# Turning the next batch's mask half a tile apart, splitting the pairs' weights on GpSimd, and signalling the rows to gather first, in a routed expert kernel

## Chip, cores and metric

The kernel runs on one core of one Trainium2 chip. The metric is device time in microseconds (us) of the whole program; the lower the better.

## What is computed

For each of 4 batches the reference builds a 1024 x 1024 matrix `adj = side * cond * softmax(x) / 32`, puts minus infinity on its diagonal, and makes a 0/1 mask of the 10240 largest entries. The mask is the input of a mixture-of-experts layer, whose output is added to `x`:

```python
out = jnp.zeros((g, n * n), dtype=adj.dtype).at[rows, idx].set(1.0)     # the mask
...
scores = jax.nn.softmax(jnp.einsum('bsh,he->bse', x, G), axis=-1)       # x is the mask here
value, indices = jax.lax.top_k(scores, TOPK)                            # TOPK = 2 of E = 8
w = jnp.einsum('bsk,bske->bse', value, onehot)
gate = jax.nn.silu(jnp.einsum('bsh,efh->bsef', x, gate_w))
up = jnp.einsum('bsh,efh->bsef', x, up_w)
out = jnp.einsum('bsef,bse,ehf->bsh', gate * up, w, down_w)
lr = jnp.einsum('bsh,erh->bser', x, lora_A)
out = out + LORA_SCALE * jnp.einsum('bser,bse,ehr->bsh', lr, w, lora_B)
```

## The kernel before

The four batches run one after the other. The 2048 pairs (token, chosen expert) of a batch are sorted by expert into T = 23 tiles of 128 slots. A tile i goes through these steps:

- GpSimd (POOL) gathers its 128 mask rows from `mask_rows` in memory to `xg` (`gather`, L509, three buffers).
- TensorE (PE) turns them (`turn_x`, L663), ScalarE (ACT) copies the turned rows to `xt` (`store_xt`, L835).
- PE does the first layer (`first_layer`, L676, 16 matmuls), ACT the silu (L840), VectorE (DVE) the gating (`gate`, L1336 to L1344), PE turns that (`turn_g`, L687), DVE copies it (`store_gt`, L1352).
- PE does the second layer (`second_layer`, L699 to L702, 8 matmuls of 512 columns in two halves), ACT copies each half to `y` (`store_y`, L848, two buffers of y, each free again when its put has landed), and POOL scatters y to `put_rows` (`put_out`, L517).

PE's order is written out by hand. In its step i stand the first layer of tile i, the turn of x of tile i + 2, the turn of g of tile i - 1 and the second layer of tile i - 2; between these are spots 0 to 3, at which tables put work for batch n + 1. ACT and DVE have spots too. Each engine works strictly down its own list, so a wait at a spot holds all that is behind it.

In the spots of batch n the mask of batch n + 1 is made, ending with `check_mask` on DVE at (18, 2), which signals `mask_ready`. SyncE (SP) then loads x for a later batch (8 loads of 512 KB to `v`) and stores the mask (2 MB, L386). From tile 19 on, the mask is turned and scored, piece c of 8 at a time: PE turns it to one PSUM bank (`turn_mask`, L625), ACT copies that to `mt` (`store_mt`, L828, two buffers), PE multiplies by the router's weights (`score`, L632). The turn of piece c + 1 waits for the copy of piece c, since there is one bank. The score of piece 7 stands behind the last tile's step and signals `scores_ready`. DVE meanwhile takes row maxima of x of batch n + 2 (L931, table MAX_AT), each of which waits for its load.

`route(n + 1)` is then one long row of small DVE instructions, with a drain between any two that depend: `choose` (L1217, waits for `scores_ready` and for the mask's store, because it writes over the mask), `weigh` (the pairs' two weights, split into three fp16 parts each), `place_pairs` (each pair's tile and slot within it), `fill_table` (L1303, 1840 values for each partition), then 16 matmuls on PE (L652), and `take_slots` (the rows to gather and to put, and the scales, of all 23 tiles), which ends in the signal `routed`. POOL issues the first gather of the next batch only behind `routed`. The first batch's route runs once before the loop.

Behind the put of the last tile, SP loads the finished rows in pieces (L362, L364); POOL sums them (L526, L529) between the tiles of the next batch.

## Time and profile before

| what | us |
|---|---|
| median of 3 runs (lowest, highest) | 834.33 (832.57, 835.94) |
| profiled execution, its own time | 836.23 |
| its span in the trace | 834.5 |
| PE busy, DVE busy, ACT busy, POOL busy | 529.9, 519.5, 455.4, 388.8 |

The span is what the instructions of the profiled execution cover; 1.7 us of its time lie around it. No engine is busy for more than two thirds of the span, so the time is in waits, and the chain of work that ended last has to be read by stages. The TensorE clock that was granted was 0.838 of full speed on the mean.

### The profile page before, as it was taken

How to read it: one execution, taken by the hardware profiler on the slowest of the kernel's cores; microseconds unless marked ns; L12 is line 12 of the kernel's file. 1: busy time of each engine (PE TensorE's matmuls, PEld its weight loads, DVE VectorE, ACT ScalarE, POOL GpSimd, SP SyncE). 2: the span in 40 equal slices, each digit the busy share in tenths (PEclk: the TensorE clock that was granted, in tenths of full speed). 3: DMA queues.
4: the chain of work that ended last, by engine and by line, in shares of the span. 5: the costliest groups of instructions: out<-in, count | busy, mean ns of one | idle time of the engine just before them, and what ended most of it. 6: DMA issues, size and time to landing. Idle time of an engine off the chain costs nothing.

```text
span 834.5 us, 14610 instructions
## 1 busy us (share of the span) xinstructions
PE 529.9 (63%) x4178; PEld 358.9 (43%) x4178; DVE 519.5 (62%) x1242; ACT 455.4 (55%) x655; POOL 388.8 (47%) x337
## 2 busy tenths in 40 slices
PE   0211376289888754787887726987788368798810
PEld 0200365156555533454555414654455146465500
DVE  5768799576778465865885676757861623233335
ACT  6686387658744564485444553874445345355510
POOL 7123200234473114487786124877871157767510
PEclk9755599589999995898899967999999869899965
DMA  9980340114232904478377734685678247767569
GB/s 315 358 234 0 115 189 26 45 55 158 88 127 86 356 28 129 147 252 288 107 263 240 319 104 148 215 287 174 212 247 334 77 131 252 268 212 264 203 234 380
DMA packets 80443, 159.93 MB, mean 192 GB/s; under 512 B 22889, under 2 KB 32105, under 8 KB 79856
## 3 DMA queue, kind: packets, MB, share of 16 engines
q1 hardware_dynamic: 59760, 108.60, 37.8%
q0 software_dynamic: 20608, 50.37, 17.3%
q8 instruction: 43, 0.70, 0.4%
q14 instruction: 32, 0.26, 0.1%
HBM read 107.53 MB, written 73.40 MB: 217 GB/s over the span
## 4 chain that ended last, share of the span: by engine, by line
DMA 19%; PE 18%; DVE 17%; issue 15%; POOL 14%; ACT 8%; DVEq 4%; SPq 3%; POOLq 1%; ACTq 0%
DMA out_dram<-piece 7%; DMA piece<-put_rows 6%; PE pa L676 5%; ACT mask L791 3%; DMA xg<-mask_rows,where 3%; POOL piece L526 3%; POOL piece L529 3%; DVE mask L1060 3%; DVE w L1166 2%; PE pb L663 2%; POOL xg L509 2%; ACT t_row L828 2%; DMA w<-put_rows 2%; PE pd L625 2%; POOL put_rows L517 2%
## 5 line engine op out<-in xcount | busy, mean ns | idle before, releaser
L676 PE MATMUL pa<-w,xt 128*128 x1472 | 203.2, 294 | 1.1 <-issue 0.9
L848 ACT ACTIVATE y<-pc,where 128x512 f32<-128x512 f32 x184 | 125.3, 687 | 104.8 <-PE pc L702 97.4
L676 PEld LDWEIGHTS pa<-w,xt 128*128 128x128 f16 x1472 | 150.7, 103 | 62.1 <-issue 14.7
L517 POOL DMA_INDIRECT put_rows<-y,where x92 | 92.5, 1005 | 151.9 <-ACT y L848 133.3
L1336 DVE SCALAR_TENSOR_TENSOR g_full<-pa,where,s_act 128x144 f32<-128x144 f32 x92 | 33.5, 365 | 197.0 <-ACT s_act L840 196.9
L509 POOL DMA_INDIRECT xg<-mask_rows,where x92 | 97.4, 1058 | 122.8 <-DVEq L1328 92.9
L835 ACT ACTIVATE xt<-pb 128x1024 f16<-128x1024 f16 x92 | 94.3, 1025 | 101.7 <-PE pb L663 98.7
L663 PE MATMUL pb<-ident,xg 128*128 128x128 f16 x736 | 61.4, 231 | 68.5 <-DMA xg<-mask_rows,where 46.2
L663 PEld LDWEIGHTS pb<-ident,xg 128*128 128x128 f16 x736 | 48.7, 104 | 80.1 <-DMA xg<-mask_rows,where 53.5
L840 ACT ACTIVATE s_act<-pa,small 128x128 f32<-128x128 f32 x92 | 33.8, 368 | 86.8 <-PE pa L676 86.8
L702 PE MATMUL pc<-lb,gt 128*128 x184 | 77.4, 420 | 0.0
L701 PE MATMUL pc<-wd,gt 128*128 x184 | 77.3, 420 | 0.0
L700 PE MATMUL pc<-wd,gt 128*128 x184 | 77.2, 420 | 0.0
L699 PE MATMUL pc<-wd,gt 128*128 x184 | 76.9, 418 | 0.2 <-issue 0.2
L526 POOL TENSOR_TENSOR piece<-piece 128x512 f32<-128x512 f32 x48 | 60.9, 1269 | 30.1 <-DMA piece<-put_rows 29.6
L791 ACT ACTIVATE mask<-v,small 128x1280 f16<-128x1280 f32 x48 | 65.1, 1356 | 7.0 <-POOL v L465 3.8
L529 POOL TENSOR_TENSOR piece<-piece 128x512 f32<-128x512 f32 x48 | 62.8, 1308 | 3.8
L931 DVE TENSOR_REDUCE small<-v 128x1 f32<-128x1024 f32 x32 | 38.4, 1213 | 16.0 <-DMA v<-in_x_dram 15.7
L1344 DVE TENSOR_TENSOR g_parts<-g_full,g_parts 128x144 f16<-128x144 f32 x92 | 43.4, 472 | 6.8
L1004 DVE TENSOR_SCALAR_CACHE_REDUCE mask<-v,small 128x1024 f16<-128x1024 f32 x36 | 45.0, 1274 | 2.8 <-POOL v L465 2.1
L1352 DVE COPY gt<-pb 128x384 f16<-128x384 f16 x92 | 32.3, 351 | 22.6 <-PE pb L687 20.9
L951 DVE SCALAR_TENSOR_TENSOR v<-v,small,t_row 128x1024 f32<-128x1024 f32 x32 | 45.4, 1457 | 0.7
(208 smaller groups left out, 880.0 us busy)
## 6 DMA issues: line engine op xcount, KB each, us to landing
piece<-put_rows SPq DMA_DIRECT2D x96, 256.0 KB
v<-in_x_dram SPq DMA_DIRECT2D x40, 512.0 KB, 9.1
piece<-in_x_dram SPq DMA_DIRECT2D x48, 256.0 KB
out_dram<-piece SPq DMA_DIRECT2D x48, 256.0 KB, 3.8
mask_rows<-mask SPq DMA_DIRECT2D x4, 2048.0 KB, 16.6
w<-put_rows SPq DMA_DIRECT2D x16, 512.0 KB, 10.2
w<-in_L_ffn_gate_w_dram SPq DMA_DIRECT2D x8, 512.0 KB, 10.2
w<-in_L_ffn_up_w_dram SPq DMA_DIRECT2D x8, 512.0 KB, 8.3
```

The source lines that it names most:

```text
L509: pool.indirect_dma_start(out=xg[:, g % NX, :], out_offset=None, in_=mask_rows[n % 2], in_offset=bass.IndirectOffsetOnAxis(ap=mask_row[n][ ...
L517: pool.indirect_dma_start(out=put_rows[n % 2], out_offset=bass.IndirectOffsetOnAxis(ap=put_row[n][:, i:i + 1], axis=0), in_=y[:, g % NY, : ...
L526: nc.gpsimd.tensor_tensor(piece[:, at, 0, :], piece[:, at, 0, :], piece[:, at, 1, :], ALU.add).then_inc(half_summed, 1)
L529: nc.gpsimd.tensor_tensor(piece[:, at, 0, :], piece[:, at, 0, :], piece[:, at, 2, :], ALU.add).then_inc(summed_piece, 1)
L663: last = pe.transpose(xt_ps[:, t, :], xg[:, g % NX, t * P:(t + 1) * P], ident[:, :])
L676: last = pe.matmul(l1[g % 2], xt[:, g % 2, t, :], w1[:, bass.ds(e, 1), t, k, :].rearrange("p o n -> p (o n)"), start=(t == 0 and k == 0), ...
L700: pe.matmul(pc[:, half, :], high, own(wd[:, bass.ds(e, 1), 1, cols]), start=False, stop=False)
L701: pe.matmul(pc[:, half, :], low, own(wd[:, bass.ds(e, 1), 0, cols]), start=False, stop=False)
L702: pe.matmul(pc[:, half, :], lora, own(lb[:, bass.ds(e, 1), cols]), start=False, stop=True).then_inc(y_done, 1)
L791: nc.scalar.activation(mask[:, cols], v_flat[:, cols], ACT.Sign, bias=t_at[k - 1], scale=-1.0, accum_out=act_cnt[:, p:p + 1]).then_inc(act ...
L835: nc.scalar.activation(xt[:, g % 2, :, :], xt_ps, ACT.Copy).then_inc(xt_ready, 1)
L848: nc.scalar.activation(y[:, g % NY, half * HALF:(half + 1) * HALF], pc[:, half, :], ACT.Copy, scale=y_scale[n][:, i:i + 1]).then_inc(y_rea ...
```

## The change

Four edits are made.

1. The turns of the next batch's mask begin at (18, 3), behind the second layer of tile 16, and go on half a tile apart; ACT gets a spot ahead of its copy of x, where the copy of the turned mask now stands in every other case. The counts on ACT keep their places (their spots are numbered one higher).
2. `weigh` computes the two weights of a token and signals; the split into three parts (3 casts, 2 subtractions) is made on POOL (`cut_weights`), between the puts of the last two tiles. `fill_table` waits for it. What doesn't depend on the probabilities is moved ahead of the wait for them.
3. `place_pairs` finds tiles from the bits of a slot number that is biased by 2^23, in place of scaling and rounding.
4. `take_slots` computes the rows to gather first and signals `rows_ready`; the scales come behind, and `routed` after them. POOL's first three gathers wait for `rows_ready` alone.

```diff
-    TURN_AT = {(19, 0): 0, (19, 2): 1, (20, 0): 2, (20, 2): 3, (21, 0): 4, (21, 2): 5, (22, 0): 6, (22, 2): 7}
-    STORE_MT_AT = dict(TURN_AT)
+    TURN_AT = {(18, 3): 0, (19, 0): 1, (19, 3): 2, (20, 0): 3, (20, 3): 4, (21, 0): 5, (21, 3): 6, (22, 0): 7}
+    STORE_MT_AT = {(18, 3): 0, (19, 0): 1, (19, 3): 2, (20, 0): 3, (20, 3): 4, (21, 0): 5, (21, 3): 6, (22, 0): 7}
...
+            def cut_weights(n):
+                at = WEIGH_STEPS * n
+                pair = w_pair.rearrange("p (c r) -> p c r", c=C)
+                pool.wait_ge(weights_ready, n + 1)
+                for k in range(PARTS):
+                    if k > 0:
+                        pool.wait_ge(weighed, at + 2 * k)
+                    nc.gpsimd.tensor_copy(vals[:, :, :, 1 + k], pair).then_inc(weighed, 1)
+                    if k < PARTS - 1:
+                        pool.wait_ge(weighed, at + 1 + 2 * k)
+                        nc.gpsimd.tensor_tensor(pair, pair, vals[:, :, :, 1 + k],
+                                                ALU.subtract).then_inc(weighed, 1)
+            cut_weights(0)
             for n in range(B):
-                pool.wait_ge(routed, n + 1)
+                pool.wait_ge(rows_ready, n + 1)
                 pool.wait_ge(mask_stored, 16 * (n + 1))
                 for i in range(NX):
                     gather(n, i)
+                pool.wait_ge(routed, n + 1)
...
-                for i in range(T - 3, T):
-                    put_out(n, i)
+                put_out(n, T - 3)
+                put_out(n, T - 2)
+                if n + 1 < B:
+                    cut_weights(n + 1)
+                put_out(n, T - 1)
...
                     silu(n, i)
+                    between(i, 0)
                     if i + 2 < T:
                         store_xt(n, i + 2)
-                    between(i, 0)
+                    between(i, 1)
...
             def weigh(n):
                 V.tensor_scalar(power, row_count, 1.0, None, ALU.max)
+                for r in range(ROLES):
+                    V.tensor_scalar(vals[:, :, r, 0], token_1, float(r * S), None, ALU.add)
                 dve.drain()
...
                 V.tensor_scalar(power, power, 2.0, None, ALU.mult)
+                dve.drain()
+                V.reciprocal(unpower, power)
                 dve.wait_ge(probs_ready, n + 1)
...
                 V.reciprocal(z_sum, z_sum)
-                dve.drain()
-                V.scalar_tensor_tensor(z_sum, z_sum, LIFT, power, ALU.mult, ALU.mult)
+                V.tensor_copy(vals[:, :, :, 4], unpower.unsqueeze(2).to_broadcast([P, C, ROLES]))
                 dve.drain()
                 pair = w_pair.rearrange("p (c r) -> p c r", c=C)
-                V.tensor_copy(pair[:, :, 0], z_sum)
-                V.tensor_tensor(pair[:, :, 1], z_sum, w_second, ALU.mult)
-                V.reciprocal(power, power)
-                dve.drain()
-                for k in range(PARTS):
-                    V.tensor_copy(vals[:, :, :, 1 + k], pair)
-                    if k < PARTS - 1:
-                        dve.drain()
-                        V.tensor_tensor(pair, pair, vals[:, :, :, 1 + k], ALU.subtract)
-                        dve.drain()
-                for r in range(ROLES):
-                    V.tensor_scalar(vals[:, :, r, 0], token_1, float(r * S), None, ALU.add)
-                V.tensor_copy(vals[:, :, :, 4], power.unsqueeze(2).to_broadcast([P, C, ROLES]))
+                V.scalar_tensor_tensor(pair[:, :, 0], z_sum, LIFT, power, ALU.mult, ALU.mult)
+                dve.drain()
+                V.tensor_tensor(pair[:, :, 1], pair[:, :, 0], w_second, ALU.mult).then_inc(weights_ready, 1)
...
-                V.tensor_scalar(n_tiles, ranks[:, C, :], 1.0 / P, (P - 1) / (2.0 * P), ALU.mult, ALU.add)
-                dve.drain()
-                V.tensor_scalar(n_tiles, n_tiles, TO_WHOLE, None, ALU.add)
-                dve.drain()
-                V.tensor_scalar(n_tiles, n_tiles, -TO_WHOLE, None, ALU.add)
+                V.tensor_scalar(n_slots, ranks[:, C, :], P - 1.0 + WHOLE, None, ALU.add)
+                dve.drain()
+                V.tensor_scalar(bits(n_slots), bits(n_slots), -P, None, ALU.bitwise_and)
...
-                V.tensor_scalar(slot_tile, slot, 1.0 / P, -(P - 1) / (2.0 * P), ALU.mult, ALU.add)
-                dve.drain()
-                V.tensor_scalar(slot_tile, slot_tile, TO_WHOLE, None, ALU.add)
-                dve.drain()
-                V.tensor_scalar(slot_tile, slot_tile, -TO_WHOLE, None, ALU.add)
-                dve.drain()
-                V.scalar_tensor_tensor(slot_in, slot_tile, -float(P), slot, ALU.mult, ALU.add)
+                V.tensor_scalar(bits(slot_base), bits(slot), -P, None, ALU.bitwise_and)
+                dve.drain()
+                V.tensor_tensor(slot_in, slot, slot_base, ALU.subtract)
...
             def fill_table(n):
+                dve.wait_ge(weighed, WEIGH_STEPS * (n + 1))
...
                 V.tensor_scalar(second_here, pair, float(S), -float(S), ALU.is_gt, ALU.mult)
+                dve.drain()
+                V.scalar_tensor_tensor(none_here, none_here, -1.0, pair, ALU.add, ALU.add)
+                dve.drain()
+                V.tensor_tensor(mask_row[n], none_here, second_here, ALU.add).then_inc(rows_ready, 1)
+                V.tensor_copy(put_row[n], none_here)
                 V.tensor_reduce(y_scale[n], slots_ps[:, :, 1:1 + PARTS], AX.X, ALU.add)
```

ScalarE's list in steps 21 and 22 of a batch, the two ahead of the route; `s_act` is the silu, `t_row` the copy of the turned mask (pieces 4 to 7), `y` the copies of a second layer's halves. Before:

```order
L840 ACTIVATE s_act<-pa,small 128x128 [waits l1_done]
L828 ACTIVATE t_row<-pd 128x1024 [waits mask_turned]
L848 ACTIVATE y<-pc,where 128x512 [waits put1,y_done]
L848 ACTIVATE y<-pc,where 128x512 [waits y_done]
L828 ACTIVATE t_row<-pd 128x1024 [waits mask_turned]
L840 ACTIVATE s_act<-pa,small 128x128 [waits l1_done]
L828 ACTIVATE t_row<-pd 128x1024 [waits mask_turned]
L848 ACTIVATE y<-pc,where 128x512 [waits put0,y_done]
L848 ACTIVATE y<-pc,where 128x512 [waits y_done]
L828 ACTIVATE t_row<-pd 128x1024 [waits mask_turned]
```

The same place with the change:

```order
L864 ACTIVATE s_act<-pa,small 128x128 [waits l1_done]
L852 ACTIVATE t_row<-pd 128x1024 [waits mask_turned]
L872 ACTIVATE y<-pc,where 128x512 [waits put1,y_done]
L872 ACTIVATE y<-pc,where 128x512 [waits y_done]
L852 ACTIVATE t_row<-pd 128x1024 [waits mask_turned]
L864 ACTIVATE s_act<-pa,small 128x128 [waits l1_done]
L852 ACTIVATE t_row<-pd 128x1024 [waits mask_turned]
L872 ACTIVATE y<-pc,where 128x512 [waits put0,y_done]
L872 ACTIVATE y<-pc,where 128x512 [waits y_done]
```

The last copy of the turned mask stood behind the y of tile 20; it now stands ahead of it, directly behind the last silu, and the seven before it are one place earlier each.

TensorE's list behind the first layer of tile 22, with the turn of the mask (`pd<-ident,mask`), the score (`pm<-gr_parts,t_row`), the turn of g (`pb<-ident,g_parts`) and the second layer's first matmul. Before:

```order
L625 MATMUL pd<-ident,mask 128x128 [waits mt_ready,mask_ready]
L625 MATMUL pd<-ident,mask 128x128 x7
L632 MATMUL pm<-gr_parts,t_row 128x24 [waits mt_ready]
L632 MATMUL pm<-gr_parts,t_row 128x24 x7
L687 MATMUL pb<-ident,g_parts 128x128 [waits gt_ready,g_ready]
L687 MATMUL pb<-ident,g_parts 128x128 x2
L625 MATMUL pd<-ident,mask 128x128 [waits mt_ready,mask_ready]
L625 MATMUL pd<-ident,mask 128x128 x7
L632 MATMUL pm<-gr_parts,t_row 128x24 [waits mt_ready]
L632 MATMUL pm<-gr_parts,t_row 128x24 x7
L699 ISA [waits y_ready,gt_ready]
```

And with the change:

```order
L649 MATMUL pd<-ident,mask 128x128 [waits mt_ready,mask_ready]
L649 MATMUL pd<-ident,mask 128x128 x7
L656 MATMUL pm<-gr_parts,t_row 128x24 [waits mt_ready]
L656 MATMUL pm<-gr_parts,t_row 128x24 x7
L711 MATMUL pb<-ident,g_parts 128x128 [waits gt_ready,g_ready]
L711 MATMUL pb<-ident,g_parts 128x128 x2
L723 ISA [waits y_ready,gt_ready]
```

The second turn and score of each step have left the place behind the turn of g and stand behind the second layer, so that a second layer lies between two turns on one side and a first layer on the other.

GpSimd's list at the end of the first batch; the put ahead of the casts is that of tile 21:

```order
L522 DMA put_rows<-y,where 2048x1024 [waits y_ready] x6
L545 CAST mask<-mask 128x16 [waits weights_ready]
L548 TENSOR_TENSOR mask<-mask 128x16 [waits weighed]
L545 CAST mask<-mask 128x16 [waits weighed]
L548 TENSOR_TENSOR mask<-mask 128x16 [waits weighed]
L545 CAST mask<-mask 128x16 [waits weighed]
L522 DMA put_rows<-y,where 2048x1024 [waits y_ready]
L514 DMA xg<-mask_rows,where 128x1024 [waits xt_turned,mask_stored,rows_ready]
```

Before, the seven puts stood together and the gather waited for `routed`; now five small instructions stand ahead of the last put.

## Rows read from the trace of the kernel before

**Rows 1.** Chain that ended last, tile 19 of batch 0: start us, us, what.

```profile
273.78 0.46 PE pb L663 x8
...
275.18 1.03 ACT t_row L828
...
277.14 0.23 PE pc L699
...
278.54 0.43 PE pc L700
```

**Rows 2.** Busy by stretch, tiles 19 to 22; columns as told below.

```profile
271.31:279.61 8.30, 6.35 (x60) 4.28 (x59) 3.64 (x7) 3.68 (x5) 1.02 (x1) 0.89 0.91 306
279.61:288.00 8.39, 6.44 (x69) 4.57 (x67) 4.75 (x8) 4.57 (x6) 0.99 (x1) 0.91 1.04 425
288.00:294.29 6.29, 5.45 (x60) 3.80 (x60) 3.51 (x7) 3.68 (x6) 0.98 (x1) 1.00 0.52 214
294.29:302.63 8.34, 5.81 (x71) 4.01 (x69) 2.62 (x7) 5.31 (x8) 1.52 (x2) 1.00 0.01 2
```

Each row is the stretch and its length, the busy time of PE, of PE's weight loads, of DVE, ACT and POOL (with their instructions), then the granted clock, the DMA engines' share and GB/s.

**Rows 3.** Timeline, TensorE: the last score and its wait.

```profile
302.28 0.36 PE L632 MATMUL pm<-gr_parts,t_row 128*128 128x24 bf16 x8 [1.70 <-ACT t_row L828]
```

**Rows 4.** Timeline: start of choose (three), tile 19's first layer in batch 1.

```profile
303.13 0.35 DVE L1217 TENSOR_REDUCE mask<-pm 128x64 f32<-128x192 f32 x1
...
445.26 2.02 PE L676 MATMUL pa<-w,xt 128*128 x16
...
477.41 0.35 DVE L1217 TENSOR_REDUCE mask<-pm 128x64 f32<-128x192 f32 x1
...
650.55 0.34 DVE L1217 TENSOR_REDUCE mask<-pm 128x64 f32<-128x192 f32 x1
```

**Rows 5.** Timeline of the route behind batch 0.

```profile
308.01 0.17 DVE L1250 SCALAR_TENSOR_TENSOR mask<-mask 128x8 f32<-128x8 f32 x1
...
310.01 0.16 DVE L1270 TENSOR_SCALAR mask<-pm 128x8 f32<-128x8 f32 x1
310.25 0.17 DVE L1272 TENSOR_SCALAR mask<-mask 128x8 f32<-128x8 f32 x1
...
313.89 2.29 DVE L1299 TENSOR_TENSOR mask<-slot_no,mask 128x2048 f16<-128x2048 f16 x1
...
319.99 0.18 DVE L1318 TENSOR_SCALAR mask<-pm 128x23 f32<-128x23 f32 x1 [0.89 <-PE pm L652]
320.08 0.17 DVE L1319 TENSOR_SCALAR mask<-pm 128x23 f32<-128x23 f32 x1
...
322.09 1.06 POOL L509 DMA_INDIRECT xg<-mask_rows,where  x1 [11.11 <-DVEq L1328]
```

**Rows 6.** Timeline of GpSimd: a chain of five small instructions, drains between.

```profile
31.86 0.24 POOL L486 CAST gr_parts<-piece 128x64 bf16<-128x64 f32 x1
...
33.50 0.24 POOL L486 CAST gr_parts<-piece 128x64 bf16<-128x64 f32 x1
```

**Rows 7.** Timeline and transfers: the mask's three stores; KB each, us to landing.

```profile
275.25 0.52 SPq L386 DMA_DIRECT2D mask_rows<-mask  x1
...
mask_rows<-mask SPq DMA_DIRECT2D x1, 2048.0 KB, 17.1
...
455.41 0.69 SPq L386 DMA_DIRECT2D mask_rows<-mask  x1
...
mask_rows<-mask SPq DMA_DIRECT2D x1, 2048.0 KB, 16.7
...
624.27 0.54 SPq L386 DMA_DIRECT2D mask_rows<-mask  x1
...
mask_rows<-mask SPq DMA_DIRECT2D x1, 2048.0 KB, 16.5
```

**Rows 8.** Timeline and transfers: gather of tile 22 in batch 1.

```profile
449.75 1.04 POOL L509 DMA_INDIRECT xg<-mask_rows,where  x1
...
xg<-mask_rows,where POOLq DMA_INDIRECT x1, 7.5
```

More of the change, by code:

```diff
@@ L195, in build @@
         picked = temp(Q * E).rearrange("p (c r e) -> p c r e", c=C, r=ROLES)
-        slot, slot_tile, slot_in = (temp(Q) for _ in range(3))
-        z_sum, w_second, power, w_pair = temp(C), temp(C), temp(C), temp(Q)
-        n_tiles, pairs_below = temp(E), temp(E * E).rearrange("p (a e) -> p a e", a=E)
-        tiles_below, tiles_to = temp(E), temp(E)
+        slot, slot_base, slot_in = (temp(Q) for _ in range(3))
+        z_sum, w_second, w_pair = temp(C), temp(C), temp(Q)
+        power, unpower = temp(C), temp(C)
+        n_slots, slots_within = temp(E), temp(E * E).rearrange("p (a e) -> p a e", a=E)
+        slots_below, slots_to = temp(E), temp(E)
         none_here, second_here = temp(T), temp(T)
@@ L288, in build @@
         mask_turned, mt_ready, scores_ready = sem("mask_turned"), sem("mt_ready"), sem("scores_ready")
-        logits_ready, probs_ready, chosen_ready, ranked, table_ready, slots_ready, routed = (
-            sem(n) for n in ("logits_ready", "probs_ready", "chosen_ready", "ranked", "table_ready",
+        logits_ready, probs_ready, chosen_ready, ranked, weights_ready, weighed, table_ready, slots_ready, routed = (
+            sem(n) for n in ("logits_ready", "probs_ready", "chosen_ready", "ranked", "weights_ready", "weighed", "table_ready",
                              "slots_ready", "routed"))
+        rows_ready = sem("rows_ready")
         gathered = [sem(f"gathered{i}") for i in range(NX)]
@@ L445, in _ @@
                                     base=0, pattern=[[1, P]], channel_multiplier=-1)
-            for ints in (expert_no, tile_no, token_1):
+            for ints in (expert_no, tile_base, token_1):
                 nc.gpsimd.tensor_copy(ints, ints.bitcast(I32))
@@ L1273, in place_pairs @@
                 dve.drain()
[L1274 removed]
+                V.scalar_tensor_tensor(slots_within, n_slots.unsqueeze(1).to_broadcast([P, E, E]), -WHOLE,
+                                       lower, ALU.add, ALU.mult)
                 dve.drain()
[L1276 to L1277 removed]
+                V.tensor_reduce(slots_below, slots_within, AX.X, ALU.add)
```

38 lines of the change are left out of this document (17 added, 21 removed).

## Prediction

> **What bounds the kernel now.** I read first the chain of waits, because no engine is busy for two thirds of the span. It goes through the same stretch three times: in tiles 19 to 22 of batches 0 to 2 it alternates between TensorE and ScalarE, then it runs down VectorE's route without a gap, through the matmuls and the row tables, to the first gather and the first turn of x. A fourth route, ahead of batch 0, is on it too. So a microsecond taken out of either part shortens the span, unless something else that doesn't move takes over.
>
> Then the busy times by stretch for tiles 19 to 22 [rows 2]. TensorE is busy for 6.35 of 8.30 us, 6.44 of 8.39, 5.45 of 6.29 and 5.81 of 8.34 us: it idles for 1.95, 1.95, 0.84 and 2.53 us, 7.3 us for the batch. The chain has ScalarE's copy of the turned mask, 1.03 us [rows 1], ahead of the turn behind each of these gaps, and the timeline says of the last score that it waited 1.70 us for the last copy [rows 3]. ScalarE is not full: 3.68, 4.57, 3.68 and 5.31 us [rows 2]. The copy comes late since in ScalarE's list it stands behind the copy of x or behind a y. The idling has a second price: the granted clock is 0.89 and 0.91 in the first two stretches against 1.00 in the last two [rows 2], and one matmul of the second layer takes 0.23 us at the upper level (2.4 GHz) and 0.43 at the lower (1.2 GHz), 1.4 us later in the same stretch [rows 1]. Tile 21, with two turns, two scores and no turn of x, costs 5.45 us of busy time; with 0.46 for the turn of x [rows 1] tiles 19 and 20 should cost 5.91, and they cost 0.44 and 0.53 more. That is 1.0 us of clock.
>
> **Edit 1, the turns.** The eight turns and scores stay; only places change. With the change every turn has a layer of the tile between itself and the next turn: either 8 matmuls of the second layer (8 x 0.23 = 1.8 us [rows 1]) or the first layer (2.0 us [rows 4]). ScalarE needs 1.03 us for the copy and starts almost at once, because the copy now stands directly behind the silu or behind the second y. Over the four tiles ScalarE has 3.68 + 4.57 + 3.68 + 5.31 = 17.2 us of work [rows 2], less than the 23 us worked out below for TensorE, so the waits can go altogether. Stretch without waits, at the upper level: 5.91 + 5.91 + 5.45 + 5.81 = 23.1 us, against 31.3 now: 8.2 us. I take 8.5, since tile 21's own first layer still began a little slow.
>
> What the shortened stretch runs into does not move with it:
> - The mask's store. `choose` waits for it. It was issued at 275.25, 455.41 and 624.27 and landed 17.1, 16.7 and 16.5 us later [rows 7], at 292.4, 472.1 and 640.8. `choose` began at 303.13, 477.41 and 650.55 [rows 4]. So at most 10.8, 5.3 and 9.8 us can be won. Puts now come earlier and share the transfers: about one more put of 0.5 MB falls ahead of the store's end in batches 0 and 2, at 425 GB/s [rows 2] 1.2 us. The caps become 9.6, about 4.5 and 8.6 us.
> - In batch 1 the gather of tile 22 is issued at 449.75, behind a sum of finished rows, and lands 7.5 us later at 457.25 [rows 8]. Tile 19 starts at 445.26 [rows 4]; with the change TensorE has turned piece 0 (0.45 us) and waited about 0.4 for `mask_ready`, starts tile 19 at 446.1 and wants the turn of x of tile 22 at 446.1 + 5.9 + 2.6 = 454.6. It waits 2.6 us there, and loses about 1 us of clock behind it: 8.5 - 0.4 - 2.6 - 1.0 = 4.5 us, the same as the cap.
>
> I take 8.5 + 4.4 + 8.5 = 21.4 us. Bounds: 14 (caps 2 us lower and some waits stay) and 24 (caps as now). The turn at (18, 3) waits for `mask_ready`; behind it on TensorE stands the first layer of tile 19. In batches 0 and 2 the second layer of tile 16 is at the lower clock and ends after the check, so it costs nothing.
>
> **Edit 2, the weights.** From L1250 to L1270 the route takes 2.00 us [rows 5]. What is left of this is one dependent step and one independent: 0.24 (L1270 to L1272) and 0.09 (L1318 to L1319) [rows 5]. That takes out 1.67. Added ahead: two independent additions (0.18), a reciprocal behind a drain (0.24) and a broadcast copy (0.09), 0.51. Net 1.16 us for each route.
>
> The split itself goes to GpSimd, and `fill_table` waits for it. Trace of before: a chain of a cast, a subtraction, and so on, five instructions of 64 columns with drains, takes from 31.86 to 33.50 + 0.24, 1.88 us [rows 6]. Here there are 16 columns and a signal in place of each drain; I take 2.0 us (1.2 to 3). The cover is what VectorE does between the weights and the table: `place_pairs`, 3.1 us after edit 3, and the 2.29 us of L1299 [rows 5], 5.4 us together. So nothing is paid. Queued behind the split on GpSimd is the put of tile 22, which can now go about 2 us later relative to the route; SP's loads of finished rows wait for it. They land well before the first sum, which stands behind the gathers of the next batch; nothing waits.
>
> **Edit 3, the tiles.** Three dependent steps fewer in `place_pairs` (one in the first rounding, two in the second), 3 x 0.24 = 0.72 us.
>
> **Edit 4, the signal.** From the start of `take_slots` to the first gather it is 2.10 us [rows 5]. With the change: 0.09 + 0.24 + 0.24 + 0.17 for four instructions, and the way from the signal to the gather. Of the 2.10, about 0.6 lies behind the last drain. So 1.35, and 0.75 us won (0.5 to 0.85). `routed` comes 0.2 us later than now, but only the fourth gather and TensorE's turn of x wait for it, and the gathered rows land over 3 us later.
>
> **Sum.** Route: 1.16 + 0.72 + 0.75 = 2.6 us, four times, 10.5 us (8 to 12). With the turns 21.4: 31.9 us. Off the profiled execution's own time of 836.2 that is 804.3; the median of the runs shown is 1.9 lower, which gives 802.4. The stretches behind (tiles 0 to 18 with the sums of finished rows) hang on the start of the batch, so I expect them to move as they are. I take off about 1.5 us for a y of tile 21 that waits for a put and holds the exponentials, which stand behind it on ScalarE: **804 us**.
>
> **The rivals.**
> - *Transfers take over.* In the stretch at 279.61 the DMA share is 1.04 at 425 GB/s [rows 2]: the transfers are full. If the earlier puts go ahead of the mask's store altogether, the caps fall by another 2 to 2.5 us in each batch: 804 + 7 = 811. For it speaks that share; against it, that the store is issued before these puts. The Trainium skill (DMA: Bandwidth & Descriptors, "Issuing engines are not separate DMA queues") says that transfers of all issuing engines run on the same 16 engines and interleave. By that rule GpSimd's earlier puts must slow SP's store; the sum with the rule is nearer to 811, without it nearer to 802.
> - *The waits stay* (the edit doesn't do what it says). ScalarE's list is in order, and a copy stands behind a y that waits for its put. If turns wait as long as now and only the last score's 1.7 us goes: 3 x 1.7 + 10.5 = 15.6, **819 us**. For it: two y buffers. Against: ScalarE's 17.2 us of work against TensorE's 23.
> - *The split isn't hidden* (the other side). Place: the wait at `fill_table`, four times. Each of the five steps costs s; nothing is paid up to 5.4 / 5 = 1.1 us a step. The kernel ends slower than before only if 4 x (5s - 5.4) is over 32 us, s over 2.7 us. At 3 us: 4 x 9.6 = 38.4, so 804 + 38 = 842. Rows of 1.88 us for all five [rows 6] speak against it.
> - *More than I count.* Batches reach the caps and the clock stays up into the route: 797.
>
> **How the numbers follow.** Forecast 0.67 (its own range 798 to 809), transfers 0.14, waits stay 0.13, split not hidden 0.03, more 0.03. Range 797 to 816, which leaves out the waits that stay and the slow case. What a measurement can tell from no change is about 0.5%, 4 us. All cases but the split end more than 4 us below 834.3, and a mild form of it would too; I leave 0.02 for no difference and 0.03 for slower.
>
> **What would show it.** After: the wait of turn 1 for ScalarE's copy gone, the last score without a wait; tiles 19 and 20 at 5.9 us and a granted clock of 1.00; `choose` beginning within a microsecond of the mask's landing; VectorE's first addition of `place_pairs` about 0.35 us behind the first weight; no wait of the table for GpSimd; the first gather some 1.35 us behind the first instruction of `take_slots`. From the first instruction of `choose` to the first gather 18.96 us now, 16.3 then. The prediction is wrong if turns still wait for copies, if the puts hold y, or if the tiles 0 to 18 of the next batch grow by what the boundary lost.

## The result, and the profile after

| what | before | with the change |
|---|---|---|
| median of 3 runs (lowest, highest) | 834.33 (832.57, 835.94) | 802.4 (796.75, 807.1) |
| span of the profiled execution | 834.5 | 794.8 |
| granted clock, mean | 0.838 | 0.851 |

The ratio is 0.9614 (95% interval 0.951 to 0.9719): 3.9% faster, 31.9 us on the medians. The forecast was 804. The profiled execution is the fastest of the three, so its 39.7 us less of span must not be read as the gain; the table below says how much of it is the change.

The page of the changed kernel, its span and its busy times:

```profile
span 794.8 us, 14572 instructions
PE 518.8 (65%) x4178; PEld 356.7 (45%) x4178; DVE 512.0 (64%) x1206; ACT 453.8 (57%) x655; POOL 393.1 (49%) x357
```

Still no engine is busy for more than two thirds. The busy times of tiles 19 to 22 of batch 0, in the columns of [rows 2]:

```profile
267.12:273.19 6.07, 6.07 (x69) 4.55 (x68) 2.96 (x7) 4.43 (x7) 1.01 (x1) 0.90 0.97 335
273.19:278.93 5.74, 5.74 (x73) 4.22 (x70) 3.70 (x8) 4.54 (x7) 0.99 (x1) 1.00 1.02 383
278.93:284.49 5.56, 5.43 (x63) 3.85 (x60) 4.53 (x9) 2.48 (x4) 0.98 (x1) 1.00 1.05 437
284.49:290.48 5.99, 5.05 (x54) 3.47 (x55) 3.33 (x7) 4.28 (x7) 0.97 (x1) 1.00 0.32 125
```

TensorE is busy for all of the first two stretches; they took 8.30 and 8.39 us and take 6.07 and 5.74. The four are 23.36 us long, where [rows 2] add up to 31.3. The first begins 3.28 us behind the mask's check (263.84), before it was 2.27 (269.04 to 271.31): the first turn now stands ahead of it.

The timeline of the changed kernel behind batch 0, from the last tile into the route and on to the first gather (start, us, engine and line, in brackets the wait and what ended it):

```profile
274.23 0.99 POOL L522 DMA_INDIRECT put_rows<-y,where  x1 [5.22 <-ACT y L872]
...
285.29 1.26 ACT L872 ACTIVATE y<-pc,where 128x512 f32<-128x512 f32 x2 [2.60 <-DMA put_rows<-y,where]
286.44 1.02 ACT L852 ACTIVATE t_row<-pd 128x1024 f16<-128x1024 f16 x1
...
287.61 0.61 PE L649 MATMUL pd<-ident,mask 128*128 128x128 f16 x8 [0.94 <-ACT t_row L852]
...
290.15 0.35 PE L656 MATMUL pm<-gr_parts,t_row 128*128 128x24 bf16 x8
290.99 0.35 DVE L1242 TENSOR_REDUCE mask<-pm 128x64 f32<-128x192 f32 x1
...
296.16 0.17 DVE L1281 SCALAR_TENSOR_TENSOR mask<-mask 128x8 f32<-128x8 f32 x1
296.49 0.16 DVE L1290 TENSOR_SCALAR mask<-pm 128x8 f32<-128x8 f32 x1
296.64 0.23 POOL L545 CAST mask<-mask 128x16 f16<-128x16 f32 x1 [1.76 <-DVE mask L1283]
297.83 0.23 POOL L545 CAST mask<-mask 128x16 f16<-128x16 f32 x1
298.55 1.00 POOL L522 DMA_INDIRECT put_rows<-y,where  x1 [0.49 <-issue]
299.91 2.29 DVE L1313 TENSOR_TENSOR mask<-slot_no,mask 128x2048 f16<-128x2048 f16 x1
302.12 2.07 DVE L1318 TENSOR_TENSOR mask<-mask 128x1840 f16<-128x1840 f16 x1
...
306.01 0.18 DVE L1333 TENSOR_SCALAR mask<-pm 128x23 f32<-128x23 f32 x1 [0.88 <-PE pm L676]
307.59 1.05 POOL L514 DMA_INDIRECT xg<-mask_rows,where  x1 [8.04 <-DVE where L1338]
```

The last score (290.15) has no wait any more; in [rows 3] it had one of 1.70 us. One turn does wait, for 0.94 us, and the two rows above it show why: ScalarE's y (tile 19) waited 2.60 us for a put to land, that of tile 17 in the first row, and the copy of the turned mask is behind that y. In the next two batches one turn waited in the same way, for 1.09 and 1.10 us. From the first weight (L1281) to the first addition of `place_pairs` (L1290) it is 0.33 us; the two rows of [rows 5] that answer to them are 2.00 apart. GpSimd's five steps take from 296.64 to 298.06, 1.42 us, and the table that needs them starts at 302.12. The first gather comes 1.58 us behind the first instruction of `take_slots`, where it was 2.10 [rows 5].

In the other two batches `choose` begins as the mask lands:

```profile
453.18 0.36 DVE L1242 TENSOR_REDUCE mask<-pm 128x64 f32<-128x192 f32 x1 [0.57 <-DMA mask_rows<-mask]
616.95 0.36 DVE L1242 TENSOR_REDUCE mask<-pm 128x64 f32<-128x192 f32 x1 [0.94 <-DMA mask_rows<-mask]
```

**The span by stages**, from the timelines of the profiled executions. A stretch goes from the first instruction of `check_mask` to the first of `choose`, a route from there to the first gather, the tiles from the first gather to the next check; the last batch ends the span. Each row is one execution.

| kernel | 4 routes | 3 stretches | tiles, and the last batch | first `choose` | span |
|---|---|---|---|---|---|
| before | 75.97 | 101.19 | 517.8 | 139.5 | 834.5 |
| changed | 68.0 | 80.77 | 507.5 | 138.6 | 794.8 |
| changed again (e0) | 69.05 | 83.59 | 514.6 | 139.4 | 806.7 |
| edit 1 alone (e1) | 81.42 | 79.8 | 515.0 | 139.5 | 815.8 |
| edits 2 to 4 alone (e2) | 65.89 | 101.27 | 516.3 | 139.2 | 822.7 |
| copies first (e3) | 76.16 | 82.75 | 519.9 | 139.0 | 817.8 |
| split on VectorE (e4) | 73.93 | 76.43 | 515.4 | 139.4 | 805.1 |
| exponentials first (e8) | 65.58 | 81.62 | 516.7 | 139.7 | 803.6 |
| split slowed (e7) | 78.36 | 77.12 | 528.8 | 139.5 | 823.8 |
| mask stored first (e6) | 65.98 | 82.58 | 517.2 | 142.9 | 808.6 |
| signal late (e9) | 70.56 | 80.87 | 510.4 | 139.0 | 800.8 |
| last gather early (e10) | 65.65 | 79.47 | 519.0 | 139.7 | 803.8 |
| split behind the put (e11) | 68.98 | 75.85 | 516.4 | 138.9 | 800.1 |
| slowed, behind the put (e12) | 81.34 | 78.93 | 517.4 | 139.0 | 816.7 |

In the changed kernel's first profile the stretches gave 20.4 us, the routes 8.0, the first `choose` 0.9. The other 10.4 us stand in the tiles and the last batch. No other kernel's tiles were as short, the same kernel's in e0 included.

### The profile page after: what moved, and what is told of

It reads as the page before. It is cut to its first block, busy times and chain, and to the rows that moved or that the text cites. A ratio compares the mean times of both kernels' runs of the same rounds, so it can differ in the third digit from the quotient of the medians.

```text
span 794.8 us, 14572 instructions
## 1 busy us (share of the span) xinstructions
PE 518.8 (65%) x4178; PEld 356.7 (45%) x4178; DVE 512.0 (64%) x1206; ACT 453.8 (57%) x655; POOL 393.1 (49%) x357
## 4 chain that ended last, share of the span: by engine, by line
DMA 25%; POOL 17%; DVE 16%; issue 15%; PE 12%; ACT 7%; DVEq 3%; SPq 2%; POOLq 1%; ACTq 0%
DMA out_dram<-piece 7%; DMA put_rows<-y,where 7%; DMA piece<-put_rows 7%; POOL piece L531 4%; POOL piece L534 4%; PE pa L700 3%; ACT mask L815 3%; DVE v L1458 2%; POOL xg L514 2%; DMA xg<-mask_rows,where 2%; POOL put_rows L522 2%; DVE w L1191 2%; ACT y L872 2%; DVE mask L1085 2%; PE pb L687 2%
## 5 line engine op out<-in xcount | busy, mean ns | idle before, releaser
L700 PE MATMUL pa<-w,xt 128*128 x1472 | 198.7, 289 | 0.9 <-issue 0.6
L700 PEld LDWEIGHTS pa<-w,xt 128*128 128x128 f16 x1472 | 146.7, 100 | 55.9 <-issue 10.5
L687 PE MATMUL pb<-ident,xg 128*128 128x128 f16 x736 | 63.1, 235 | 68.9 <-DMA xg<-mask_rows,where 48.5
L723 PE MATMUL pc<-wd,gt 128*128 x184 | 75.5, 411 | 5.0 <-ACT y L872 4.9
L724 PE MATMUL pc<-wd,gt 128*128 x184 | 75.0, 408 | 0.0
L725 PE MATMUL pc<-wd,gt 128*128 x184 | 74.7, 406 | 0.0
L726 PE MATMUL pc<-lb,gt 128*128 x184 | 74.3, 404 | 0.0
L531 POOL TENSOR_TENSOR piece<-piece 128x512 f32<-128x512 f32 x48 | 61.1, 1272 | 25.8 <-DMA piece<-put_rows 25.3
L1360 DVE TENSOR_TENSOR g_parts<-g_full,g_parts 128x144 f16<-128x144 f32 x92 | 47.3, 514 | 7.5 <-issue 0.9
L976 DVE SCALAR_TENSOR_TENSOR v<-v,small,t_row 128x1024 f32<-128x1024 f32 x32 | 42.8, 1375 | 0.6
L711 PE MATMUL pb<-ident,g_parts 128*128 128x128 f16 x276 | 32.4, 230 | 13.6 <-DVE gt L1368 13.5
```

The lines of the kernel that those rows point to most:

```text
L531: nc.gpsimd.tensor_tensor(piece[:, at, 0, :], piece[:, at, 0, :], piece[:, at, 1, :], ALU.add).then_inc(half_summed, 1)
L687: last = pe.transpose(xt_ps[:, t, :], xg[:, g % NX, t * P:(t + 1) * P], ident[:, :])
L700: last = pe.matmul(l1[g % 2], xt[:, g % 2, t, :], w1[:, bass.ds(e, 1), t, k, :].rearrange("p o n -> p (o n)"), start=(t == 0 and k == 0), ...
L723: pe.matmul(pc[:, half, :], high, own(wd[:, bass.ds(e, 1), 0, cols]), start=True, stop=False)
L724: pe.matmul(pc[:, half, :], high, own(wd[:, bass.ds(e, 1), 1, cols]), start=False, stop=False)
L725: pe.matmul(pc[:, half, :], low, own(wd[:, bass.ds(e, 1), 0, cols]), start=False, stop=False)
```

## The experiments

Each ratio is to the kernel before, run beside it on the same chip. Runs e1 to e4, then e0 and e6 to e8, then e9 to e12 were made on three different chips, so between these groups only ratios are compared. The diffs show the lines that matter; where ScalarE's copies move, the spot ahead of its copy of x and the renumbered counts come with them.

**e1, edit 1 alone**, and **e2, edits 2 to 4 alone.** Before's code with the first edit, and the changed code with before's places:

```diff
-    TURN_AT = {(19, 0): 0, (19, 2): 1, (20, 0): 2, (20, 2): 3, (21, 0): 4, (21, 2): 5, (22, 0): 6, (22, 2): 7}
+    TURN_AT = {(18, 3): 0, (19, 0): 1, (19, 3): 2, (20, 0): 3, (20, 3): 4, (21, 0): 5, (21, 3): 6, (22, 0): 7}
```

> Edit 1 alone (turns and copies of the next batch's mask) on the kernel before. My theory: the stretch from the mask's check to the start of choose falls from 34.1, 32.9, 34.2 us to some 27.2, 26.5, 27.2 as in the changed kernel, capped by the landing of the mask's store, and the route keeps its 19 us. Time: 834.3 - 20 = 814 us. Rival (the turns help less than the sum says, the route edits bring more): 820 or above.

> Edits 2 to 4 alone, with the turns and copies at the places of before. My theory: the route (first instruction of choose to first gather) is 16.3 us each time, without the two routes of 17.5 us that the changed kernel showed, since the y of tile 21 no longer waits for a put; the stretch stays at 33 to 34 us. Time: 834.3 - 4 x 2.6 = 824 us. Rival: the tiles 0 to 18 of a batch, which came out 1.4 to 3.3 us shorter in the changed kernel's profile, depend on the route's edits; then 818 us.

e1 took 813.9 us, ratio 0.9777 (0.9721 to 0.9833); e2 821.57, ratio 0.9862 (0.9806 to 0.9918). In e1's profile the stretches gave 21.4 us together, but two of its routes were longer than before's, 21.93 and 21.45 us. The waits of e1 behind batch 1 (engine and line, what for, total us, times, longest):

```profile
DVE mask L1245 <- ACT mask L884: 3.0, 1, 3.0
ACT y L848 <- DMA put_rows<-y,where: 2.8, 1, 2.8
```

`weigh` (L1245) waited 3.0 us for the exponentials, which stand on ScalarE behind a y that waited 2.8 us for its put. Before, the stretch was long enough for that put to land. In e2 the stretches were as before, 101.27 against 101.19, and its routes took 16.26, 16.63, 16.65 and 16.35 us: 10.1 us less, all of it in the route. The two gains, 2.2% and 1.4%, add up to about the whole. The rows of e2 also tell edits 2 to 4 apart, as means over four routes: from the first of `choose` to the first of `place_pairs` 1.23 us less (edit 2), from there to the comparison with the slots (L1312 in e2, L1299 before) 0.68 less (edit 3), from the first of `take_slots` to the first gather 0.62 less (edit 4). Alone, edit 1 gives a quarter of what it wins in the stretches back in the routes (5.5 of 21.4 us).

**e3, the copies first.** Before's kernel with before's turns; only the copies of the turned mask come earlier in ScalarE's list.

```diff
-    STORE_MT_AT = dict(TURN_AT)
+    STORE_MT_AT = {(19, 0): 0, (19, 1): 1, (20, 0): 2, (20, 1): 3, (21, 0): 4, (21, 1): 5, (22, 0): 6, (22, 1): 7}
```

> The kernel before with TensorE's turns at their old places; only ScalarE's copies move: the even ones directly behind the silu, the odd ones directly behind the copy of x, ahead of both y. Theory A (the late copy in ScalarE's list is the cause of the waits): turns still stand close together on TensorE, so some 0.4 us of wait is left at each second turn and the last score waits for nothing; the stretch falls by 5 to 6 us, time 817 to 820. Rival B (the turns must lie apart on TensorE): the stretch falls by 2 us or less, time 828 or above.

818.48 us, ratio 0.9804 (0.9722 to 0.9885). The timeline of e3, TensorE's turns of the mask, and its last score:

```profile
276.26 0.61 PE L625 MATMUL pd<-ident,mask 128*128 128x128 f16 x8 [0.59 <-ACT t_row L828]
...
282.30 0.61 PE L625 MATMUL pd<-ident,mask 128*128 128x128 f16 x8 [0.39 <-ACT t_row L828]
...
288.34 0.61 PE L625 MATMUL pd<-ident,mask 128*128 128x128 f16 x8 [0.84 <-ACT t_row L828]
...
294.96 0.61 PE L625 MATMUL pd<-ident,mask 128*128 128x128 f16 x8 [1.22 <-ACT t_row L828]
...
297.33 0.35 PE L632 MATMUL pm<-gr_parts,t_row 128*128 128x24 bf16 x8
```

Four waits of 0.39 to 1.22 us are left of the idling, and the stretch is 6.1 us shorter on the mean; with the turns moved too it is 6.8 (changed kernel) or 7.1 (e1). The last of the four stands behind a y that waited 2.37 us for its put. So the place of the copy in ScalarE's list is most of the cause, and half a tile between turns the smaller part. In time e3 and e1 can't be told apart.

**e4, the split on VectorE.** The changed kernel with the casts and subtractions back in `weigh`.

```diff
+                dve.drain()
+                for k in range(PARTS):
+                    V.tensor_copy(vals[:, :, :, 1 + k], pair)
+                    if k < PARTS - 1:
+                        dve.drain()
+                        V.tensor_tensor(pair, pair, vals[:, :, :, 1 + k], ALU.subtract)
+                        dve.drain()
```

The calls of `cut_weights` and the wait in `fill_table` are left out.

> The changed kernel with the three-part split back on VectorE, everything else as changed. Theory: from the first weight's instruction to the first one of place_pairs 0.33 us becomes about 1.6 us, the route 1.3 us longer each time, the kernel 5 us slower than the changed one (807 to 808). Rival (the split on GpSimd delays the last put and through it the finished rows, which costs what it wins): no slower than the changed kernel, 802.

807.15 us, ratio 0.9704 (0.9641 to 0.9767). The first route, which meets no wait for exponentials, took 17.48 us against 16.25. VectorE's rows of e4 behind batch 0, from the first weight to the first addition of `place_pairs`:

```profile
298.29 0.17 DVE L1278 SCALAR_TENSOR_TENSOR mask<-mask 128x8 f32<-128x8 f32 x1
...
299.88 0.16 DVE L1294 TENSOR_SCALAR mask<-pm 128x8 f32<-128x8 f32 x1
```

1.59 us, where the changed kernel has 0.33: the split costs 1.23 to 1.26 us for each route when VectorE does it, and nothing on GpSimd. Four times that is 5 us; the ratios of this kernel and e0 differ by 0.73%, 6 us, though their intervals still overlap.

**e0, the changed kernel again**, beside the next three.

> The changed kernel once more, to see what of its first profile is chance. Theory: the stretches from check to choose come out the same to half a microsecond (27.2, 26.4, 27.2), the routes too (16.3 to 17.7), and the tiles 0 to 18 with the last batch, 507.5 us in that profile against 515 to 520 in those of five other kernels with the same tiles, come out nearer to 515, so the span near 803. Rival: the tiles' gain belongs to the change; 507 again and a time of 797.

808.95 us, ratio 0.9631 (0.9601 to 0.966), with a median of 839.87 for before on that chip. The tiles and the last batch came back to 514.6 us. Over the eleven experiments other than e7 they are 516.2 us on the mean, before 517.8: of the 10.4 us most was chance of that one execution, and the 1.6 us between the means is less than the profiles differ among themselves. The span came out at 806.7 where 803 was expected. The stretches did not repeat to half a microsecond either, 28.42, 30.69 and 24.48 us. Of the second, the timeline of e0:

```profile
435.25 5.04 SPq L331 DMA_DIRECT2D v<-in_x_dram  x8
...
435.68 1.04 POOL L514 DMA_INDIRECT xg<-mask_rows,where  x1
...
445.31 0.93 PE L687 MATMUL pb<-ident,xg 128*128 128x128 f16 x7 [4.48 <-DMA xg<-mask_rows,where]
```

The gather of tile 22 went out 0.43 us behind the loads of x and took until 445.3; TensorE's turn of x waited 4.48 us for it. In the changed kernel's first profile this wait was not there.

**e8, the exponentials first.** ScalarE's exponentials for the route stand ahead of the y of tile 21.

```diff
+                probabilities(n + 1)
                 store_y(n, T - 2, 0)
                 store_y(n, T - 2, 1)
-                probabilities(n + 1)
```

> The changed kernel with the exponentials of the route ahead of the y of tile 21 in ScalarE's list. Theory: in the changed kernel's batches 1 and 2 that y waited 2.8 and 3.0 us for its put and held the exponentials, for which VectorE then waited; with the exponentials first all four routes are 16.3 to 16.6 us, 2.4 us less in all: 800. Rival: the y, held instead by the exponentials, delays the last puts and the finished rows, and the time stays or grows to 804 to 806.

805.9 us, ratio 0.9598 (0.9574 to 0.9623). The four routes took 16.25, 16.52, 16.59 and 16.22 us, 10.4 less than before, and none waits for ScalarE. Its ratio is the lowest here, and its time 3 us below that of e0 beside it, but the intervals overlap: the wait is shown gone, the gain in time only likely.

**e6, the mask stored first.** SP's store of the mask goes out ahead of the eight loads of x; its own wait moves with it and is not shown.

```diff
+                sp.dma_start(mask_rows[n % 2].rearrange("(p c) h -> p (c h)", c=C),
+                             mask[:, :]).then_inc(mask_stored, 16)
...
-                sp.dma_start(mask_rows[n % 2].rearrange("(p c) h -> p (c h)", c=C),
-                             mask[:, :]).then_inc(mask_stored, 16)
```

> The changed kernel with SyncE issuing the mask's store ahead of the eight loads of x. Theory (choose waits for the store's landing in batches 1 and 2): the store lands 8 us or more ahead of choose, whose waits of 0.6 and 0.9 us for it go; but the rows of x land some 4 us later, and VectorE's maxima, which stand ahead of the gate in its list, wait for them and hold the gate in batches 0 and 1; the stretches there grow by 1 to 3 us, the last one shrinks by 1; time 801 to 806. Rival (transfers are the bound of the whole stretch, whatever their order): stretches within 0.5 us of the changed kernel's.

810.96 us, ratio 0.9663 (0.963 to 0.9697). `choose` no longer waits for the mask in any batch, but VectorE waits longer for the rows of x. The waits of e6 in the stretch behind batch 0, then behind batch 1:

```profile
DVE small L956 <- DMA v<-in_x_dram: 6.8, 4, 3.7
...
DVE small L956 <- DMA v<-in_x_dram: 8.0, 2, 7.8
```

In e0 beside it VectorE had none of these waits behind batch 0, and 6.7 us of them, the longest 4.6, behind batch 1 (before: 6.8 and 5.1). These maxima stand ahead of `choose` on VectorE. In front of the first `choose` it waited 5.8 us for x (0.4 in e0), and `choose` came at 142.9 us, not 139. One late transfer took the place of another: the wait for the mask can be taken away by order, but this order won no time. Whether another would was not tried.

**e7, the split slowed.** The changed kernel with nine memsets and drains on GpSimd ahead of the last cast; they do no work of the kernel.

```diff
+                    if k == PARTS - 1:
+                        for _ in range(9):
+                            nc.gpsimd.memset(scratch[:, :], 0.0)
+                            pool.drain()
```

> The changed kernel with nine small memsets, a drain behind each, put into GpSimd's split ahead of its last cast, some 3.5 us, so that the split takes about 5 us in place of 1.4, still less than the 5.7 us from the last weight to the table on VectorE. They write an unused buffer. Theory (the split is covered, and the last put may go later): routes as in the changed kernel, at most 0.3 us longer, the time the same, 802 to 803. Rival (the later put of tile 22 and the finished rows behind it count): 4 us for each of three batches less what is slack, 806 to 814.

825.85 us, ratio 0.983 (0.9795 to 0.9865), 17 us above e0: more than theory and rival had. The timeline of e7 behind batch 0:

```profile
305.80 1.23 POOL L546 MEMSET scratch<- 128x64 f16 x5 [3.82 <-issue]
...
308.51 2.08 DVE L1323 TENSOR_TENSOR mask<-mask 128x1840 f16<-128x1840 f16 x1 [2.19 <-POOL mask L550]
309.01 2.45 POOL L523 DMA_INDIRECT put_rows<-y,where  x1 [0.54 <-issue]
...
312.73 0.33 SPq L368 DMA_DIRECT2D piece<-in_x_dram  x1
...
314.00 1.06 POOL L515 DMA_INDIRECT xg<-mask_rows,where  x1 [2.54 <-DVE where L1343]
...
320.90 1.01 PE L692 MATMUL pb<-ident,xg 128*128 128x128 f16 x8 [8.53 <-issue]
```

The padding cost more than its size, for GpSimd paused 3.82 us among the memsets: the split took 7.7 us, not 5, and the table waited 2.19 us. But what the three routes behind a batch lost, 2.5 to 5.2 us each against the 16.6 us of the first profile, is not all. The last put left at 309.01 and SP, which waits for it, began to load finished rows at 312.73, just ahead of the first gather at 314.00. From that gather to the first turn of x it was 6.9 us; in e0, 3.6 (its rows follow). Behind batches 1 and 2 it was 7.1 and 7.5. The tiles grew too, to 528.8 in the table, the only kernel over 520: 12.6 us above the mean of the others, of which these three late turns are some 10.7.

```profile
314.42 1.05 POOL L514 DMA_INDIRECT xg<-mask_rows,where  x1 [8.05 <-DVE where L1338]
...
318.02 1.01 PE L687 MATMUL pb<-ident,xg 128*128 128x128 f16 x8 [5.22 <-issue]
```

**e12, the slowed split behind the last put**, to take the collision away and keep the padding:

```diff
-                if n + 1 < B:
-                    cut_weights(n + 1)
                 put_out(n, T - 1)
+                if n + 1 < B:
+                    cut_weights(n + 1)
```

> The padded split, now behind the put of tile 22 (ScalarE's list as in the changed kernel). With the padding ahead of the put the gather issued at 314.00 brought its turn of x only at 320.90, 6.9 us later against 3.6 us in the unpadded kernel, since SyncE's loads, held by the put, were issued 1.3 us ahead of it. Theory (the loads of finished rows collide with the first gathers): with the put ahead, the loads are issued 6 us or more before the gathers, the first turn of x comes 3.6 us behind its gather again and the tiles 0 to 18 take 114, 118 to 119 and 120 us in place of 114, 125.7 and 123; the table still waits for the split, routes 19 us or more. Time 6 to 10 us below the padded one, ratio 0.972 to 0.977. Rival (it is the padding itself, not the put): tiles as in the padded kernel, 0.983.

825.16 us, ratio 0.9862 (0.9816 to 0.9909); the time expected was missed, it is no lower than e7's. The timeline of e12 at the same place, then its wait of the table:

```profile
305.24 0.33 SPq L368 DMA_DIRECT2D piece<-in_x_dram  x1
...
317.18 1.09 POOL L515 DMA_INDIRECT xg<-mask_rows,where  x1 [5.54 <-DVE where L1343]
...
320.79 1.01 PE L692 MATMUL pb<-ident,xg 128*128 128x128 f16 x8 [5.25 <-issue]
```

```profile
DVE mask L1323 <- POOL mask L550: 3.8, 1, 3.8
```

The loads go 12 us ahead of the gather, and from the gather to the turn it is 3.6 us again with the padding still there (3.6 and 3.7 behind the other batches). So it was not the padding itself that made the turn late, but when the loads came; e10 below shows the same without any padding. The tiles of this profile are at 517.4, but it is the fastest of five executions, 6.8 us below their median, so that number proves little. The split now begins behind the put, the table waits 3.8 us, and the routes behind a batch take 21.3 to 21.8 us. That these 3.0 us more of routes are all that keeps the median at e7's is not shown.

**e11, e8 with the split behind the last put**, with no padding. The edit is that of e12.

> Exponentials first, and GpSimd's split behind the put of tile 22 in place of ahead of it. Theory: the split then ends some 2 us later, still before VectorE reaches the table (1.4 us of split against about 4 us left), so routes stay at 16.3 to 16.6; SyncE's loads of the finished rows start up to 1 us earlier relative to the route, which is free as long as they don't meet the first gathers: the same ratio as with the exponentials first, 0.960. Rival: the put's wait for y pushes the split past the table, routes 17.5 and more, ratio 0.965.

808.21 us, ratio 0.966 (0.962 to 0.9699). Its wait behind batch 0:

```profile
DVE mask L1318 <- POOL mask L545: 0.7, 1, 0.7
```

This is what the rival said. With the put, its wait and its 1.0 us of issue, ahead of the split the table waits 0.7 us, and the three routes take 17.4 to 18.0 us where e8's take 16.2 to 16.6. The split belongs where the change has it.

**e9, the signal late.** `rows_ready` is given where `routed` is, behind the scales.

```diff
-                V.tensor_tensor(mask_row[n], none_here, second_here, ALU.add).then_inc(rows_ready, 1)
+                V.tensor_tensor(mask_row[n], none_here, second_here, ALU.add)
...
+                dve.sem_inc(rows_ready, 1)
```

> The changed kernel with the signal for the rows to gather given only behind the scales, where the whole table is done (edit 4's order kept, its early signal undone). Theory: from the first instruction of take_slots to the first gather 1.58 us becomes 2.5 to 2.6, routes 17.2 where the changed kernel has 16.25 and 16.6, 3 to 4 us in all; against the changed kernel's repeat (ratio 0.963 to before) a ratio of 0.967. Rival (the gathers' landing is set by the transfers behind them): the same ratio.

811.38 us, ratio 0.9702 (0.9654 to 0.9751), above e0's 0.9631, with intervals that overlap. The timeline of e9:

```profile
309.29 0.18 DVE L1333 TENSOR_SCALAR mask<-pm 128x23 f32<-128x23 f32 x1 [0.89 <-PE pm L676]
...
311.58 1.05 POOL L514 DMA_INDIRECT xg<-mask_rows,where  x1 [8.85 <-DVEq L1344]
```

2.29 us against 1.58: the early signal is worth 0.71 us, where 0.9 to 1.0 was expected. The first two routes, 16.97 and 17.34 against 16.25 and 16.6, say 0.72 and 0.74.

**e10, e8 with the gather of tile 22 a step earlier**, ahead of a sum of finished rows on GpSimd.

```diff
-                    if i + NX < T:
+                    if i + NX < T - 1:
                         gather(n, i + NX)
+                    if i == T - 1 - NX - 1:
+                        gather(n, T - 1)
```

> Exponentials first, and GpSimd issues the gather of the last tile in its step 18, ahead of a sum of finished rows, in place of step 19. Theory: where the gather of tile 22 is issued behind SyncE's loads of x it lands 7 to 10 us later and TensorE waits for it (4.5 us in batch 1 of the changed kernel's repeat, none in its first profile); issued some 5 us earlier it lands in 4 to 5 us, and no stretch is above 28.5. Time 2 to 3 us below the kernel with the exponentials first alone, ratio to before 0.956 to 0.958. Rival (chance, and the wait only moves): 0.960.

806.92 us, ratio 0.9634 (0.9594 to 0.9673), beside 0.9598 for e8: no gain that can be told. TensorE waited for no gather in any of the three stretches. In e8's profile that wait was not there in batch 1 either, only 1.56 us of it in batch 2. The stretches are 2.2 us shorter together than e8's, as expected, and `choose` then waited 1.0 us for the mask's landing. Further on some 4.2 us were lost. The timeline of e10 behind batch 2:

```profile
639.34 0.34 SPq L367 DMA_DIRECT2D piece<-in_x_dram  x1
...
640.72 1.05 POOL L514 DMA_INDIRECT xg<-mask_rows,where  x1 [2.53 <-DVE where L1340]
...
647.67 1.01 PE L689 MATMUL pb<-ident,xg 128*128 128x128 f16 x8 [8.57 <-issue]
```

The put of tile 22 went late here, the loads of finished rows came 1.4 us ahead of the first gather, and the first turn of x 6.95 us behind it, with no padding on GpSimd. Behind batch 1 the loads came 3.3 us ahead and the turn 4.5 behind. In all the other profiles but e7's the first of these loads came at least 5.6 us ahead, and the turn followed in 3.5 to 3.75 us. Why the put was late is not shown. Behind one limit of the stretch stands the next.

## Why the prediction was right

- **The chain and its price.** Right. Most of TensorE's idling in tiles 19 to 22 was the wait for ScalarE's copies (e3), and the clock came back with it, but for tile 19 of batch 0: 0.90, 1.00, 1.00 and 1.00 there (before 0.89, 0.91, 1.00, 1.00), and 1.00 in all four tiles of batches 1 and 2. "Tiles 19 and 20 at 5.9" were 6.07 and 5.74. The four stretches without waits, 23.1 in the prediction, took 23.36, 0.94 of it the wait of a turn, and 22.6 and 22.7 in batches 1 and 2.
- **Edit 1, 21.4 us.** Right in sum, and in part by luck. It was 20.4 in the changed kernel's first profile, 21.4 in e1, and over the eleven profiles that have the edit from 17.6 (e0) to 25.3 (e11), 21.5 on the mean; three of them lie above the bounds 14 to 24. But the prediction made it up of 8.5, 4.4 and 8.5 us, and the first profile has 6.9, 6.5 and 7.0 (means of the eleven: 7.8, 5.7 and 8.0): too much at the ends and too little in the middle cancel. Batch 1 won more because the gather of tile 22 was not waited for, which was to cost 2.6 us and 1.0 of clock; in e0 it was, for 4.48 us. The ends won less for two reasons. The turn at (18, 3) was to cost nothing in batches 0 and 2, but from the check to tile 19 it is 1.0 and 0.7 us longer than before (1.95 in batch 1, where 0.8 was taken). Behind that, one turn of each batch waited for a copy held by a y, and in batch 2 `choose` waited for the mask. The caps were named rightly: in batches 1 and 2 `choose` began 0.1 us behind the mask's landing.
- **The transfers.** The mask's stores took 18.0, 18.0 and 18.8 us to land, against 17.1, 16.7 and 16.5 in [rows 7]: 0.9, 1.3 and 2.3 us more, where the term had 1.2. The prediction had taken one more put ahead of the store's end; the rival's 2 to 2.5 us on top of that came in no batch, though in batch 2 the cap came at 7.0 us, not 8.6. The Trainium skill (DMA: Bandwidth & Descriptors, "Issuing engines are not separate DMA queues") says that transfers interleave whichever engine starts them; the stores agree, by these 0.9 to 2.3 us. In e2, with before's turns, they took 17.6, 16.6 and 15.8 us.
- **A term that was mis-sized: puts that hold ScalarE.** The prediction took off 1.5 us for a y of tile 21 that waits for its put and holds the exponentials. In the changed kernel that put held y by 2.8 and 3.0 us behind batches 1 and 2, and VectorE waited 1.0 and 1.2 us, 2.2 together; in e0 one route took 19.6 us where 16.6 is the length without such a wait, and in e1, which lacks the instructions that edit 2 puts ahead of the wait, two routes were 3.3 and 2.2 us longer than before's. A wait of the same kind inside the stretch was not counted: y of tile 19 waited 2.60 us for a put that took 11.0 us, and a turn lost 0.94 us, 1.09 and 1.10 in the other batches. So two of the prediction's own signs of being wrong, turns that wait for copies and puts that hold y, did appear, at a price that the sum could bear. e8 takes the first part away for nothing.
- **Edit 2, 1.16 us a route.** Right: 1.23 by the rows of e2. The split takes 1.42 us on GpSimd, not 2.0, and hides with 4 us to spare. That it would not hide was given 3 in 100; e7 shows what it costs then.
- **"Nothing waits" for the later last put.** Right for the change, where the put goes out at 298.55 and the gather at 307.59, and wrong as a general step. When the put is late enough for SP's loads to go out 1.3 to 1.4 us ahead of the first gather, the first turn comes 3.3 to 3.9 us later (e7, and e10 once), and with the loads earlier it doesn't (e12).
- **Edit 3, 0.72, and edit 4, 0.75.** Edit 3 was not run by itself; the rows of e2 give it 0.68 us. Edit 4 was mis-sized: from `take_slots` to the first gather it is 1.58 us, not 1.35, behind each batch, so 0.52 us won, and 0.90 only in the first route (2.60 to 1.70). By e9 the early signal is worth 0.71, since the late one now stands behind more instructions than before. The route as a whole says 2.5 us for edits 2 to 4 (e2: 10.1 us in four; 10.4 in e8), predicted 2.6. The route of 18.96 us, "16.3 then", took 16.6.
- **The sum.** 28.4 us by the stretches and routes of the first profile (its first `choose`, 0.9 us earlier, was at 139.4 again in e0), 31.0 us by e0's ratio and its before's 839.87, 31.9 by the first medians; predicted 30.4. That tiles 0 to 18 move as they are holds on the mean: in the eleven experiments other than e7 the tiles and the last batch take 510.4 to 519.9 us, before 517.8.

What stays open is what moves that stage by some 10 us from one execution to the next; no run here aimed at it. A third buffer for y, which might take the puts' waits away, was not tried.

## What to carry to other kernels

A wait of an engine that works down a fixed list is often the wrong order on the engine it waits for: look there first, for moving the copies alone (e3) gave 6.1 of the 6.8 us that moving copies and turns gave. When a stretch gets shorter, list for each engine what was hidden by its length (here two puts, one store, one gather), and put what the next stage needs ahead of anything that waits for a transfer. When work that releases bulk loads moves later, look at what those loads will then meet: here 1.4 us ahead of the first gather cost over 3 us, 5.6 us ahead nothing. Compare sums of stages over several profiles before crediting a change with a stage it didn't touch.

## What was not expected of the hardware

- A stage whose code stays the same varies by more than edits 2 to 4 win together: tiles and last batch from 507.5 to 519.9 us over thirteen profiles (e7 apart), and one stretch of the changed kernel between 26.44 and 30.69 us. That kernel's time varied between 796.75 and 813.04 us over its two measurements.
- GpSimd paused for 3.8 us in a row of short memsets with drains (e7; 3.9 in e12), where nothing that the profile shows held it.
- One put of 0.5 MB took 11.0 us to land while the mask's store was under way, at a DMA share of 1.02 and 1.05 in the two stretches that it mostly lies in, where the median of this kernel's puts is 3.7.
